# Second attention of a two-layer kernel: the next batch's preparation in slots of seven heads instead of six

## What is computed

```python
q = _split_heads(layernorm(x) @ Wq.T, 8)          # 512 x 32 for each head
k, v = _split_heads(ctx @ Wk.T, 8), _split_heads(ctx @ Wv.T, 8)   # 1601 x 32
attn = softmax(einsum('bhnd,bhmd->bhnm', q, k) * 32 ** -0.5)
x = x + merge_heads(einsum('bhnm,bhmd->bhnd', attn, v))
```

## Time and profile before

| | us |
|---|---|
| median of 3 runs | 2890.53 (2888.62 to 2890.86) |
| the profiled execution, its own time | 2888.98 |
| its span, first to last instruction | 2887.1 |
| PE busy | 2487.0 (86%) |
| DVE busy | 1947.3 (67%) |
| ACT busy | 1661.8 (58%) |
| POOL busy | 1553.2 (54%) |
| mean granted TensorE clock, share of full speed | 0.934 |

### The profile page before, as it was taken

How to read it: one execution, slowest core, us unless ns; L and a number is a source line. 1 busy time by engine, 2 the same in 40 slices (tenths; PEclk the granted TensorE clock), 3 DMA queues, 4 the chain that set the end, 5 groups by cost and what they waited for, 6 DMA issues and landing times. The chain is left out here.

```text
span 2887.1 us, 46961 instructions
## 1 busy us (share of the span) xinstructions
PE 2487.0 (86%) x15253; PEld 1504.2 (52%) x15380; DVE 1947.3 (67%) x3548; ACT 1661.8 (58%) x2669; POOL 1553.2 (54%) x1400
## 2 busy tenths in 40 slices
PE   4999999999999999999973797169999999279992
PEld 2455555555555555555532686135555544268882
DVE  5778677786777867777755643558888887655443
ACT  3555655566555565555541753047878788167661
POOL 3576766767667676666684001626867689310004
PEclk9999999999999999999985899589999999579996
DMA  4000000000000000000005521220202010743113
GB/s 125 9 1 1 24 1 1 1 1 24 1 1 1 1 1 1 1 1 1 1 12 183 183 64 49 75 68 2 68 2 68 2 46 1 242 160 95 47 44 95
DMA packets 87109, 122.90 MB, mean 43 GB/s; under 512 B 12418, under 2 KB 71636, under 8 KB 86932
## 3 DMA queue, kind: packets, MB, share of 16 engines
q1 hardware_dynamic: 75604, 86.23, 10.0%
q0 software_dynamic: 9472, 30.16, 3.0%
q10 hardware_dynamic: 1856, 4.19, 0.4%
HBM read 73.23 MB, written 34.34 MB: 37 GB/s over the span
## 5 line engine op out<-in xcount | busy, mean ns | idle before, releaser
L396 POOL TENSOR_TENSOR a_acc<-a_acc,a_pf 128x512 f32<-128x512 f32 (+1 forms) x480 | 639.1, 1332 | 388.8 <-ACT a_pf L524 368.6
L1831 POOL TENSOR_TENSOR c_pl<-c_pf,c_ph 128x512 f16<-128x512 f32 x320 | 378.1, 1210 | 173.0 <-ACT c_ph L1930 172.8
L524 ACT ACTIVATE a_pf<-a_psS 128x1024 f32<-128x1024 f32 (+1 forms) x288 | 281.2, 976 | 304.1 <-PE a_psS L663 300.6
L813 DVE TENSOR_TENSOR a_pl<-a_pf,a_ph 128x512 f16<-128x512 f32 x448 | 420.1, 947 | 28.5 <-ACT a_ph L530 28.5
L789 DVE TENSOR_REDUCE a_mx<-a_psA 128x1 f32<-128x512 f32 x512 | 342.8, 684 | 46.0 <-PE a_psA L600 41.0
L1270 POOL DMA_INDIRECT f_xn<-f_yrows,f_gidx x64 | 60.6, 947 | 506.4 <-DMA f_yrows<-f_xn 487.6
L530 ACT ACTIVATE a_ph<-a_psS 128x1024 f16<-128x1024 f32 (+1 forms) x288 | 281.0, 976 | 0.0
L2158 DVE TENSOR_REDUCE c_mx<-c_psA 128x1 f32<-128x512 f32 x384 | 250.9, 685 | 34.6 <-PE c_psA L2001 32.7
L1923 ACT ACTIVATE c_pf<-c_psS 128x1024 f32<-128x1024 f32 x192 | 197.7, 1030 | 89.8 <-PE c_psS L2033 88.9
L1130 DVE TENSOR_TENSOR f_xn<-f_xn 128x256 f16<-128x256 f32 x320 | 132.4, 422 | 131.1 <-ACT f_xn L1106 127.2
L784 DVE TENSOR_TENSOR a_vl<-a_psA,a_vh 128x256 f16<-128x256 f32 (+1 forms) x272 | 115.1, 423 | 155.6 <-ACT a_vh L469 152.7
(11 more groups left out here) (321 smaller groups left out, 6387.3 us busy)
## 6 DMA issues: line engine op xcount, KB each, us to landing
f_stage<-in_L_ffn_w SPq DMA_DIRECT2D x16, 1024.0 KB, 5.6
f_stage<-in_L_ffn_W SPq DMA_DIRECT2D x16, 1024.0 KB, 5.6
f_xn<-f_xrows SPq DMA_DIRECT2D x41, 256.0 KB, 2.7
f_yrows<-f_xn SPq DMA_DIRECT2D x40, 256.0 KB, 2.2
c_kst<-c_khs SPq DMA_DIRECT2D x64, 100.1 KB, 2.2
f_xrows<-f_zero POOLq DMA_DIRECT2D x1, 6400.0 KB, 27.0
a_cx<-in_ctx SPq DMA_DIRECT2D x4, 1536.0 KB
c_cx<-in_ctx SPq DMA_DIRECT2D x12, 512.0 KB, 4.0
```

Of the source, the lines that this page charges most:

```text
L396: g.tensor_tensor(acc[0:k, p, :], acc[0:k, p, :], pf[0:k, q % RF, i, :], ALU.add).then_inc(s_acc, 1)
L524: act.activation(pf[0:r, q % RF, 0:k, :], psS[q % 2][0:r, 0:k, :], ACT.Exp, scale=SCALE).then_inc(s_pF, 1)
L813: v.tensor_tensor(pl[0:r, q % RP, i, :], pf[0:r, q % RF, i, :], ph[0:r, q % RP, i, :], ALU.subtract).then_inc(s_pL, 1)
L1831: g.tensor_tensor(pl[0:r, q % RP, i, :], pf[0:r, q % RF, i, :], ph[0:r, q % RP, i, :], ALU.subtract).then_inc(s_pG, 1)
```

## The change

The slots are taken from heads 0 to 6 instead of 0 to 5. There are then 26 slots for the 25 items.

```diff
     M_AT = [(0, 0), (0, 2), (0, 3), (1, 0), (1, 2), (2, 0), (2, 2), (2, 3), (3, 0), (3, 2), (4, 0), (4, 2)]
-    PREP_AT = [(h, u, p) for h in range(6) for u, p in ((1, 1), (4, 1), (5, 1), (6, 1))]
+    PREP_AT = [(h, u, p) for h in range(7) for u, p in ((1, 1), (4, 1), (5, 1), (6, 1))]
     PREP_AT = [(h, u, p) for h, u, p in PREP_AT if (h, u) >= (0, LAG + 1)]
```

## The result

| | before | changed |
|---|---|---|
| median us (lowest to highest, 4 runs each) | 2889.57 (2888.60 to 2890.86) | 2907.21 (2904.63 to 2911.37) |
| ratio to before, 95% interval | | 1.0062 [1.0045, 1.008] |
| span of the profiled execution | 2887.1 | 2907.0 |
| mean granted clock | 0.934 | 0.932 |

The change makes the kernel slower by 17.6 us, 0.62%. The forecast was +29, 2919 us, with a range of 2906 to 2932.

What follows compares the result with a forecast made beforehand. PE was taken to bound stage C. Late context 9.7 + 10.8, third passage 8.7, clock 2 x 1.5, less 2 (spread) and 1 (hole), gave +29.2 on 2889.0: 2918.2, named 2919 us; range 2906 to 2932.

Steps and rivals of the forecast that it cites:

- What bounds the stage: Stage C: PE bounds it, and an item costs about what PE spends on it wherever it stands.
- the signs: Expected in the profile: four copy waits, three context waits, head 7 about 21 us, heads 1 and 2 a little shorter.
- Part 3: First M of head 7: PE waits 3.9 to 5.4 us for the late copies, plus 3.3 of low clock.
- Part 4: First T after batches 0 and 1: context 9.7 and 10.8 us late, containing the M's loss; 1.5 us clock each.
- Part 1: Loaded heads: one more head hides 0.7 us a batch, -2 us in all, between 0 and -4.
- Part 2: Head 3, PE waiting for DVE's norm: the hole shrinks by 0.4 us three times, -1 us; its whole price 6.8.
- A: The new waits come but the clock does not fall behind them: +23, about 2913 us; chance 0.14.
- B: Each new wait costs its own low clock in full, the spread gives nothing: +36, about 2927 us; chance 0.11.
- C: No slower: the hole of head 3 goes altogether, leaving +4 us, within 0.2%; chance 0.03.
- D: Copies are issued before the last Q, so PE gets the M's operands in time: -3 us; chance 0.02.

Runs made afterwards that it cites:

- e6: Kernel before, with the norm's four instructions put one each behind units 1, 2, 4 and 5 of head 3; 2871.6 us, -18.4 to before.
- e4: Kernel before, with only the two Q items moved late, to units 4 and 5 of head 6; 2916.4 us, +27.0 to before.
- e3: Changed kernel, with the V items of the last three units put behind the Q items; 2878.9 us, -10.5 to before.
- e8: Changed kernel with late V items behind the Q items, context loads ahead of the copies and the norm split; 2854.9 us, -35.1 to before.
- e7: Changed kernel, with the norm split into four pieces in head 3; 2895.4 us, +5.3 to before.
- e9: Kernel before, with context loads ahead of the copies and the norm split; 2861.4 us, -28.0 to before.
- e2: Changed kernel, with the next batch's first two context loads issued ahead of the 48 copies; 2890.6 us, +1.2 to before.
- e5: Changed kernel, with the 24 key copies of a stack issued ahead of the wait for the last Q (batch 0 as before); 2891.5 us, +1.5 to before.
- e1: Kernel before, with the next batch's first two context loads issued ahead of the 48 copies; 2880.3 us, -9.1 to before.

## Why the prediction was right, and where it was not

**What bounds the stage.** Right. No new wait of PE longer than 0.2 us appeared in the three batches that was not named, and the busy time by head follows PE. Of the signs, one failed: head 1 was not shorter (18.4 for 18.3), because the low clock behind the wait at the T reached into it.

**Part 3, the first M.** Right in place and mechanism, and in the idle time: the wait was 3.9 us three times, the lower end of 3.9 to 5.4. The clock was taken at 3.3 and was 3.25 (7.15 - 3.90), but that agreement is in part luck. Its source was head 3, where 3.5 us were put down to the low clock; by e6 the price of that hole was 5.8, so 2.5. And in e4 the same wait cost 2.4 us of clock in two of three batches. At the third passage I had put 8.7 us, for the slower landings and issues seen in the trace; it was 7.2. Sum 21.5 instead of 23.1 (7.2 + 7.2 + 8.7). e4 and e3 show that it hangs on the last Q: put it late alone and the loss comes, put it early alone and it goes.

**Part 4, the context.** Right in mechanism and in the arrival. The first T started at t + 38.4 against t + 38.7. After the wait at the M, 2.1 us were left to wait instead of 2.5 and 3.6. The low clock behind it was put at 1.5 us and was larger: the stretch with the T lasts 18.23 us against 14.80 in e8, the one after it 18.43 against 17.17, so 3.4 + 1.3 = 4.7, of which 2.1 are the wait and 2.6 the clock. Two of them are 9.4 against 9.1 forecast. That the sum agrees is luck: the wait was put too high (6.1 for 4.2) and the clock too low (3.0 for 5.2), and in e4 and e7 one such wait each passed without any fall of the clock.

**Part 1, the spread.** This is the term that was mis-sized: "one more 0.7 us can hide: -0.7 us a batch". It measured -7 in three batches, not -2, beyond the bound of -4. The term took what a head hides as a constant per loaded head. The runs show that it depends on which items stand in the head: heads 1, 2 and 4 went from 18.26, 18.35 and 18.38 us to 17.17, 17.38 and 15.84 (e9 to e8, where the order of the last items differs too) and in the changed kernel's own order head 4 went to 17.0, while head 6 rose from 15.1 to 16.4. Put together from the runs where each head has no wait for a transfer or the whole norm (heads 0 to 2 of e2; 3 to 6 of e7), that order gives 2.3 us a batch, so the -7 is not owed to the late V of e8. The busy time by head had a sign of it: head 1 hid 0.7 of its 5.2 us, head 2 with two K in one place only 0.3 of 4.8.

**Part 2, the hole.** The idle time was right (2.80 instead of 3.25, 0.45 less; 0.4 forecast). The whole price of the hole was put at 6.8 us and is 5.8 by e6. The step that failed is the price of the change, which counted only the idle time: "The hole shrinks by 0.4 us, three times, -1 us". With it the low clock behind it shrank, and the hole's cost fell by 6.4 us, not 1. Why a hole smaller by an eighth leaves a head at 0.92 instead of 0.79 was not settled: in the changed kernel all three batches had 22.4 us in head 3, while in e2 and e3 the same hole of 2.80 us gave 22.4 in the first batch and 23.5 in the other two, and in e5 22.4 twice and then 23.5. So some of the 6.4 us may belong to where the hole fell in this trace and not to its size.

**The rest.** In batch 0 the context wait, which both kernels have, was 1.3 us shorter in the changed one (9.29 against 10.59): in the profiled execution of before, one issue took 1.59 us instead of 0.59 and another 0.87. The edit touches neither. But it may not be chance: the three kernels with six heads of slots that have this wait (before, e4, e6) had such a slow issue there and waited 10.6, 10.4 and 9.8 us, the four with seven (changed, e3, e5, e7) had none and waited 9.0 to 9.3. On the other side e1 and e9, with six heads, had none either in batch 0. The cause stays open.

**The sum.** 21.5 + 9.4 - 7 - 6.4 - 1.3 = +16.2, where the trace has 445.7 us instead of 428.4 from the first head's hand-over (L2165) to the one 24 heads on, so +17.3. The 1.1 us that are missing are batch 0's second head, which stands behind the opening's wait for the context at a lowered clock: it had 18.4 us in the changed kernel, where 17.2 is its time without that. (The profiled spans differ by 19.9; 1.7 of the rest stand ahead of the first hand-over, where e1 and e9, kernels with six heads of slots, also come 0.8 to 1.9 us later than before, and 0.9 behind these heads.) The forecast's +29.2 was too high by 11.9: 5.0 in part 1, 5.4 in part 2, 1.6 in part 3 and 1.3 in batch 0's wait, less 0.3 in part 4 and the 1.1 just named. The new waits alone, 30.9 us against 32.2, were within 2 us. (2918.2 and 1.5 make 2919.7, so 2919 was rounded down.) That the time still lies in the range is in part luck: the low end was reckoned from a clock that does not fall, part 1 at -4 and a hole half mended. The clock did fall, and what brought the time down there was the spread, beyond its stated bound, and the cheaper hole.

**The rivals.** A fell in its mechanism: in the changed kernel's trace the clock went down behind each new wait. Its 2913 is nearer to the 2907.2 measured than my 2919, by luck. B fell in its sizes, though its claim of a low clock of its own at the T was right. C asked that head 3's hole go altogether; it did not, but its cost fell by more than a third without going. D fell with the four waits.

## What to carry to other kernels

Work that is spread further back ends later: before it is moved, ask what its last item releases, and count the whole chain behind it on the queue that carries it (here 6 issues of 0.64 us and a landing for the next head, 48 and a landing for the next context). If something must be late, let it be what nobody has waited for yet: the same seven heads with the values last, the context ahead of the copies and the norm cut into pieces are 1.2% faster than the kernel before. A hole on TensorE is to be priced with the low clock behind it, and as a range: here that clock cost nothing behind two waits of 2.3 and 2.9 us, and 2.4 to 3.3 behind waits of 3.9.

## What the runs showed of the hardware

- In head 7, which prepares nothing, PE waits of 3.9 us were followed by 3.2 to 3.3 us of loss at the lower clock in all three batches of the changed kernel and in the first of e4, and by 2.4 in the other two of e4. Waits of 1.94 us (e5) were followed by 2.2 to 2.5, and the two of 2.1 us at the first T of the changed kernel by 2.6 each.
- Not every such wait lowered the clock: behind 2.89 us in e4 and 2.25 us in e7, both at a first T, it stayed at 1.00. The pauses of up to 0.8 us in e8 and e9 left it at 1.00 too. The length of the wait alone does not tell which; what else decides was not settled.
- The same 2.80 us of idle PE left head 3 at 22.4 us in some batches and at 23.5 in others of one execution (e2, e3, e5).
- Issues of small copies on SP went out every 0.64 us, with in most stacks one or two of 0.9 to 2.0 us. In batch 0 they moved the context's arrival by 1.3 us between the kernel before and the changed one.
